# Quartering the first image's arrival: four transfers of 32 partitions in place of three of 128, and the first cell sums moved between the steps of a small dependent chain

## The reference

```python
# layer 0: a gate from image 0 assigns a DCT filter to each channel; every channel is then scaled by y
g = einsum('nchw,oc->nohw', x, wg1)                     # 1x1 convolution, 32 outputs
g = relu((g - bn2_m) * (bn2_g / sqrt(bn2_v + EPS)) + bn2_b).mean(axis=(2, 3))
xg0 = (relu(tanh(g @ wg2.T + bg2)) + beta)[0]           # image 0 alone
p_mid = round(xg0[:31] / xg0.sum() * c)                 # channel ranges of the 32 filters
filt[ch] = basis[i] where param[i] <= ch < param[i + 1]
xp = x.reshape(n, c, 7, 8, 7, 8).mean(axis=(3, 5))      # 7x7 cells of 8x8 pixels
y = relu(batchnorm(sum(xp * filt) @ w1d[:, :, 1].T + b1d))
x = x * y + x
# layer 1: depthwise 3x3 convolution whose weights come from the image's own channel means
t = relu(gamma * (x.mean(axis=(2, 3)) @ w1.T - running_mean) * rsqrt(running_var + EPS) + beta)
wt = (t @ w2.T + b2) * MASK                             # MASK keeps up-left, up, up-right and left
out = conv(x, wt, padding=1, groups=b * c) + bias
```

## Time and profile before

| what | value |
|---|---|
| time, median of 3 runs (lowest to highest) | 246.6 us (245.93 to 246.85) |
| the profiled execution's own time | 245.07 us |
| its span in the trace | 242.8 us |
| PE busy | 210.7 us, 87% |
| DVE busy | 199.3 us, 82% |
| ACT busy | 132.2 us, 54% |
| POOL busy | 129.5 us, 53% |
| moved by DMA | 79.05 MB, mean 326 GB/s |
| share of the chain that ended last: PE, DVE, DMA, ACT | 69%, 10%, 9%, 6% |

### The profile page before, as it was taken

One profiled execution on the slowest core, in us unless ns is written; L12 is line 12 of the kernel. 1 busy time (PEld: TensorE's weight loads), 2 busy tenths in 40 slices (PEclk: granted clock), 3 DMA queues, 4 the chain that ended last, 5 costly groups with the idle time before them and its releaser, 6 DMA issues.

```text
span 242.8 us, 2387 instructions
## 1 busy us (share of the span) xinstructions
PE 210.7 (87%) x742; PEld 120.9 (50%) x742; DVE 199.3 (82%) x215; ACT 132.2 (54%) x190; POOL 129.5 (53%) x121
## 2 busy tenths in 40 slices
PE   7134517759999999999999999999999999999991
PEld 3011214735565566555655565556565556555550
DVE  6000089589989999999999999999999999789983
ACT  2000101145578747866677667766768676776750
POOL 3000042488986897787878697868886810040000
PEclk9855555559999999999999999999999999999999
DMA  1999999931699999999999999999998563536666
GB/s 40 229 244 237 407 426 432 424 160 85 195 366 405 370 417 380 426 413 407 397 432 430 362 417 430 428 337 422 424 427 353 246 267 165 231 132 264 264 267 262
DMA packets 8103, 79.05 MB, mean 326 GB/s; under 512 B 988, under 2 KB 1020, under 8 KB 2076
## 3 DMA queue, kind: packets, MB, share of 16 engines
q1 hardware_dynamic: 8092, 78.92, 83.1%
HBM read 40.38 MB, written 38.54 MB: 325 GB/s over the span
## 4 chain that ended last, share of the span: by engine, by line
PE 69%; DVE 10%; DMA 9%; ACT 6%; issue 3%; SPq 1%; DVEq 0%; ACTq 0%
PE banks L738 57%; DMA xout<-x 9%; DVE banks L549 6%; ACT banks L624 3%; PE banks L723 2%; PE banks L730 2%; PE banks L711 2%; PE banks L709 2%; DVE xout L549 1%; DVE stats L425 1%; PE banks L686 1%; PE banks L674 1%; ACT diag L619 1%; PE banks L701 1%; PE banks L717 1%
## 5 line engine op out<-in xcount | busy, mean ns | idle before, releaser
L738 PE MATMUL banks<-xin,diag 128*128 128x385 f32 (+1 forms) x480 | 171.1, 507 | 3.0 <-ACT banks L624 2.7
L738 PEld LDWEIGHTS banks<-xin,diag 128*128 128x128 f32 x480 | 88.3, 191 | 68.4 <-issue 27.1
L339 POOL TENSOR_TENSOR halves<-xin 128x1568 f32<-128x1568 f32 (+2 forms) x22 | 74.1, 3370 | 59.2 <-DMA xin<-x 37.1
L549 DVE SCALAR_TENSOR_TENSOR banks<-xin,coef,banks 128x1485 f32<-128x1485 f32 x48 | 84.9, 1768 | 7.0 <-ACT banks L624 6.4
L624 ACT ACTIVATE banks<-xin,wide_sb,coef 128x784 f32<-128x784 f32 (+2 forms) x71 | 84.3, 1207 | 10.0 <-DVE xout L558 8.5
L549 DVE SCALAR_TENSOR_TENSOR xout<-xin,coef,banks 128x1485 f32<-128x1485 f32 x24 | 42.2, 1758 | 0.4
L645 ACT ACTIVATE xout<-banks 128x784 f32<-128x784 f32 x24 | 19.8, 824 | 39.5 <-PE banks L738 39.5
L344 POOL TENSOR_TENSOR halves<-halves 128x784 f32<-128x784 f32 x18 | 33.2, 1846 | 1.4
L619 ACT ACTIVATE diag<-wide_sb,coef 128x128 f32<-128x128 f32 x72 | 23.4, 389 | 6.7 <-DVE coef L484 6.7
L558 DVE SCALAR_TENSOR_TENSOR xout<-xin,coef,banks 128x825 f32<-128x825 f32 x24 | 25.6, 1067 | 1.0 <-PE banks L738 0.8
L686 PE MATMUL banks<-xout,gate_w 128*128 128x392 f32 x12 | 8.9, 899 | 13.3 <-DMA xout<-x 13.3
(11 more groups left out here) (72 smaller groups left out, 85.0 us busy)
## 6 DMA issues: line engine op xcount, KB each, us to landing
xin<-x SPq DMA_DIRECT2D x23, 1568.0 KB, 10.9
out<-xout SPq DMA_DIRECT2D x23, 1568.0 KB, 13.4
xout<-x SPq DMA_DIRECT2D x3, 392.0 KB
xin<-x SPq DMA_DIRECT2D x1, 1120.0 KB, 28.4
out<-xout SPq DMA_DIRECT2D x1, 756.0 KB, 3.2
wide_sb<-wide SPq DMA_DIRECT2D x1, 499.5 KB, 26.9
xin<-x SPq DMA_DIRECT2D x1, 448.0 KB, 27.9
out<-xout SPq DMA_DIRECT2D x1, 420.0 KB, 3.3
```

The lines of the kernel that those rows point to most:

```text
L339: eng.tensor_tensor(halves[:, j % 2, 0:end, :], cells[:, :, 0, :], cells[:, :, 1, :], ALU.add).then_inc(once_folded, 1)
L549: return vec.scalar_tensor_tensor(out=to, in0=grid(k)[:, irows, cols], scalar=weight(k, which), in1=d_rows[:, :, ocols], op0=ALU.mult, op1 ...
L738: return mm(to, diag[:, k % 2, which, :], grid(k)[:, irows, cols], start=False, stop=(which == LEFT), skip_group_check=True)
```

## The change

Image 0 is cut otherwise. Before, one transfer brought one t for all 128 partitions (the HBM side walks four quarters j, then 32 channels q); now one transfer brings one quarter j for 32 partitions with all three t (the HBM side walks 32 channels q, then t). The bytes and their places in SBUF are the same. The gate product can't begin with the first t any more, since each t needs all four quarters: PE waits for all four. On DVE the wait for tile 0 and its sums go ahead of and between the steps of the channel assignment.

```diff
-    x_image0 = x[0, :, :, :].rearrange("c h w -> c (h w)").rearrange("(q t) (j f) -> t j q f", t=PER, j=GROUP)
+    x_image0 = x[0, :, :, :].rearrange("c h w -> c (h w)").rearrange("(q t) (j f) -> j q t f", t=PER, j=GROUP)
...
-        image0_in = [sem(f"image0_in_{t}") for t in range(PER)]
+        image0_in = [sem(f"image0_in_{j}") for j in range(GROUP)]
...
-            for t in range(PER):
-                sp.dma_start(image0[:, t, :], x_image0[t]).then_inc(image0_in[t], 16)
+            for j in range(GROUP):
+                sp.dma_start(image0[QUAD * j:QUAD * (j + 1), :, :], x_image0[j]).then_inc(image0_in[j], 16)
...
+            dve.wait_ge(loaded[0], 16)
+            sum_direct(0, 0, 4)
             dve.wait_ge(gate_tanh, 1)
             vec.tensor_scalar(xg[:, :], gate_act[:, :], 0.0, gate_par[0:NF, 5:6], ALU.max, ALU.add).then_inc(xg_done, 1)
+            sum_direct(0, 4, 5)
             dve.wait_ge(s_mm, 1)
...
             vec.tensor_scalar(count[:, :], share[:, :], ROUND, -ROUND, ALU.add, ALU.add).then_inc(counted, 1)
-            dve.wait_ge(loaded[0], 16)
-            sum_direct(0, 0, 4)
+            sum_direct(0, 5, DCT).then_inc(cells_done, 1)
             dve.wait_ge(narrow_in, 16)
...
-            sum_direct(0, 4, DCT).then_inc(cells_done, 1)
...
+            for j in range(GROUP):
+                pe.wait_ge(image0_in[j], 16)
             for t in range(PER):
-                pe.wait_ge(image0_in[t], 16)
                 for half in range(2):
```

## The result

| | before | changed |
|---|---|---|
| time, median (lowest to highest) | 246.26 us (243.54 to 246.85), 4 runs | 230.31 us (229.69 to 230.65), 4 runs |
| ratio of the times, 95% interval | | 0.937 (0.930 to 0.944) |
| profiled execution, own time; span | 245.07; 242.8 us | 229.69; 227.5 us |

On two other occasions, beside the experiments, the changed kernel gave 230.48 us (ratio 0.942, 0.937 to 0.947) and 230.23 us (0.939, 0.933 to 0.945). The forecast was 228.7 us, between 226.0 and 235.5: the time lies in the range, 1.6 us above the forecast, and just above the 226.4 to 230 that the forecast gave its own case. Medians and extremes here count every execution; the ratios leave out the few that took over 1.5% longer than the fastest of their kernel.

A forecast was written before the change was run, and what follows sets the result against it. Image 0 on four DMA engines was taken to delay the convolution's start: landing 8.95, `xg` 15.1, `chosen` 19.4, first sums 24.7, convolution 33.9 instead of 51.85; gain 17.9 from 246.6 gives 228.7 us, range 226.0 to 235.5.

The forecast's parts named there:

- its own case: The main forecast, chance 0.68: 228.7 us, own range 226.4 to 230, with image 0 there at 6.65 to about 9.5 us.
- image 0 on sixteen engines: Image 0's transfers in the head: 32 partitions each run on sixteen DMA engines, not four; share near 1.
- its rate: Image 0's transfers: 14 GB/s on each of sixteen engines, 220 GB/s, 5.5 us; bounds 379 and 160 GB/s.
- landing L: Image 0 there at 1.65 + 1.8 + 5.5 = 8.95 us (6.65 to 10.95), where it was at 25.77.
- gate product: PE behind image 0's landing: all twelve MATMULs at full clock, 4.3 us, 1.3 more behind the landing than before.
- end of gate to `xg`: DVE's stretch from the gate product's end to `xg`: 1.84 us, unchanged.
- `xg` to `chosen`: DVE's channel assignment: reordered cell rows shorten it from 6.71 to 4.3 us.
- `chosen` to the first product of the sums: ACT's copy, the filters and the warming products ahead of L709: 5.27 us as before.
- that to the convolution: From the first product of the sums to the convolution: 9.28 us, left as it was.
- Rivals 2 to 5: Low rate of first 25 us, 0.08; spread doesn't come, 0.05; half gain lost in steady part, 0.05; no change, 0.02.
- Rival 1: Late or cold gate: image 0 at 10.95 us, gate product 8.9 us at half clock; 235.3 us, chance 0.12.
- The tests of the loads: Whether tile landings keep up in the head: tile 0 at 12.7 us, tile 3 at 25.3; loss 0 to 1 us.

The follow-up runs named there:

- experiment 1: Changed kernel with DVE's cell sums back in their old order, so only the transfers and the gate product's waits are changed: 233.53 us, ratio 0.951 to the kernel before.
- experiment 8: The changed kernel itself, unaltered, measured again beside other runs on their chip: 230.48 us, ratio 0.942 to the kernel before.
- experiment 5: Changed kernel with quarters 2 and 3 of image 0 issued from the scalar engine's queue: 229.62 us, ratio 0.935 to the kernel before.
- experiment 4: Changed kernel with seven warming products in place of one ahead of the gate product: 229.91 us, ratio 0.940 to the kernel before.
- experiments 6 and 7: Changed kernel with image 0 in twelve transfers by t and quarter: on one queue 229.86 us (ratio 0.937), on sync and scalar queues 228.66 us (0.932).
- Experiment 3: Kernel before, with SP waiting for all of image 0 ahead of the first tile: 238.55 us, ratio 0.976 to the kernel before.
- the ten products: Ten products on zeros ahead of the convolution: changed kernel 229.94 us, kernel before 245.32, changed with two queues and `warm(7)` 228.21.

## Why the prediction was right, point by point

| step | forecast | profile after |
|---|---|---|
| image 0 on sixteen engines | share near 1 | 1.03 to 1.13 from 4 to 9 us |
| its rate | 220 GB/s | 198 to 276, 157 in the first us |
| landing L | 8.95 us | 10.09 (gate product begins) |
| gate product | 4.3 us, full clock | 6.79, clock 0.50 until 15.3 us |
| end of gate to `xg` | 1.84 | 1.80 |
| `xg` to `chosen` | 4.3 | 4.35 |
| `chosen` to the first product of the sums | 5.27 | 5.26 |
| that to the convolution | 9.28 | 7.93 |
| convolution begins | 33.9 us | 36.22 |
| profiled own time | 227.2 us | 229.69 |

The mechanism held: the four engines, the landing as the root of the head's chain, the steady part that moves with the convolution. Rivals 2 to 5 didn't come. Rival 1, a late and cold gate, came in part, and its two halves are the two terms that came out too small.

*The landing.* I wrote a fixed part of 1.8 us, from a transfer of 29.6 KB that runs alone, and 5.5 us for the bytes, so that they would be through at about 8.7. In the trace's transfer records the bytes of image 0 run from 3.12 to 9.19 us, 198 GB/s from end to end, and the first 0.6 us are slow (75 to 125 GB/s in windows of 0.25 us from 3.0 to 3.75). The 215 GB/s of the windows count a little of `narrow_sb` and tile 0 besides. The last completion event comes at 9.96 and PE starts at 10.09. So of the 1.1 us, about 0.5 are the bytes and 0.6 the way from the last byte to the product.

*The clock.* This is the step of the sum whose reasoning, and not only its size, failed. I took two things as given: that the clock falls at 10.4 us as before, and that a product which begins at full clock keeps it, because PE is then busy. The fall came at 8.5 in this profile (0.76 on average from 8 to 9 us: half of it at 1.00, half at 0.50), when PE had been idle since 5.9; the product began at half clock and stayed there until 15.3: 6.79 us, 2.5 more than forecast. In the two further profiles of the changed kernel it took 5.88 and 5.85 us, and 7.20 in experiment 1: the moment of the fall differs from run to run. And a start ahead of the fall doesn't help: in experiment 8 the product began at 10.01, in experiment 5 at 9.39, both at full clock, and the clock fell at 10.55 and 9.90 all the same, after PE had been idle for 3.5 and 2.9 us; both took 5.88 us. With PE kept busy up to the product (experiment 4) it is 4.19. The rows held a warning. The windows print a clock of 1.00 where the trace has no clock record, and the records begin only at 7.03 us before and at 5.11 now. The two MATMULs of warming tell what PE really had: 1.51 us before, the pace of the half clock, and 0.87 here. So the clock had risen about 1.9 us earlier in this profile, and fell 1.9 us earlier.

*The way from the sums to the convolution* was 1.35 us shorter. PE's clock was at half all through this stretch before (0.50 from 43 to 52 us); here it rose at 29.0 us, after PE had been busy since 24, stayed at 1.00 until 32.4, and the small products between ran faster. I had left this stretch as it was, so this gain is luck.

The sum of the three is +1.1 + 2.5 - 1.35 = 2.3 us, the 2.3 by which the convolution came later than forecast. The profiled time is 2.5 us above its forecast, the median only 1.6: I had added 1.5 us for the median above the profiled execution, as the three runs before had it, and it was 0.6. That the median came so near is luck to that extent.

The tests of the loads held nearly: tile 0's cell rows began at 13.99 (12.7 was forecast for the landing, 1.1 of the difference again image 0's), early enough for an `xg` that itself was late. With the gate at full clock, in experiment 4, DVE waited 0.99 us for tile 3, the 0 to 1 us that I had taken as nothing; with a still earlier gate product the four cell rows of tile 0 were the bound as well, as experiments 6 and 7 show.

What stays open: why image 0 on four engines slows the tiles on the other twelve (244 GB/s in all, where 100 alone and 423 behind it), and whether the 215 GB/s of a quarter come from the 32 partitions. Experiment 3 shows that the first effect exists, not its place. Open, too, is how much of a gain in the head the clock takes back on average: the profiles show one execution each.

## What to carry to other kernels

Read the DMA share and the rate of a transfer that is alone. Here 0.24 at 91 GB/s told of four engines at full speed before any edit, and a walk with 32 rows outermost put it on sixteen; a badly spread transfer costs more than its own time, because it slows what is beside it. Once such a wait is gone, count what stands close behind it (tile 0, the gate product's clock, tile 3): of later gains of 2.5 to 6.8 us at the gate only 0.4 to 1.8 reached the time. And a head that ends a little earlier doesn't start the dense part at full clock: in every profile here without the ten products its first 3.0 to 6.1 us ran at 1.2 GHz, so part of a gain can be spent there.

## What the runs showed of the hardware that I had not expected

- Transfers on four of sixteen engines, at 100 GB/s alone, fell to 56 GB/s when loads ran on all sixteen, and together they moved only 240 GB/s, where the loads alone move 419 to 439.
- The time from the start of the dense work to the rise of PE's clock differs between executions: 3.0, 6.1 and 4.1 us in three profiles of the changed kernel (starts at 36.22, 35.20 and 36.58 us, rises at 39.2, 41.3 and 40.7), and the first 26 MATMULs took 10.56, 12.08 and 11.11 us.
- A matrix product that begins at full clock can still lose it: with PE idle for 3.5 us ahead of it, the clock fell 0.5 us into the product (experiment 8).
- With ten products on zeros that start an accumulation in unused columns of a PSUM bank the output was not the reference's in any of three kernels; they wrote nothing in the columns that the convolution uses.
